# The edge network's first product in float32, from the attributes as they are, with the bias in a row of ones

## The reference

```python
e = jax.nn.relu(ea @ ee_w1 + ee_b1) @ ee_w2 + ee_b2     # ea: 100000 x 64, ee_w1: 64 x 256
msg = x[src] + e
agg = jax.ops.segment_sum(msg, dst, num_segments=n)
```

## Time and profile before

| | value |
|---|---|
| median of three runs | 3226.73 us (3221.56 to 3228.65) |
| profiled execution, and its span | 3227.56 us, 3225.7 us |
| PE busy | 2512.0 us, 78% |
| VectorE (DVE) busy | 2228.2 us, 69% |
| ScalarE (ACT) busy | 1485.7 us, 46% |
| GpSimd (POOL) busy | 2020.3 us, 63% |
| mean granted TensorE clock | 0.903 |
| edge stage, first gather to last | 94.4 to 1098.5 us |

### The profile page before, as it was taken

How to read it: one execution, slowest core, us unless ns; L and a number is a source line. 1 busy time by engine, 2 the same in 40 slices (tenths; PEclk the granted TensorE clock), 3 DMA queues, 4 the chain that set the end, 5 groups by cost and what they waited for, 6 DMA issues and landing times. The chain is left out here.

```text
span 3225.7 us, 81208 instructions
## 1 busy us (share of the span) xinstructions
PE 2512.0 (78%) x25602; PEld 2184.7 (68%) x25603; DVE 2228.2 (69%) x4515; ACT 1485.7 (46%) x3803; POOL 2020.3 (63%) x2143
## 2 busy tenths in 40 slices
PE   0577777777778699999999999965777777777773
PEld 0466666666666589999999999964555555555552
DVE  7687778778777546666666666657666667766666
ACT  5344444444444377888888888841111111111113
POOL 4677777777777534444444444427777777777772
PEclk9998899889888899999999999987998888879886
DMA  6555555555555400000000000006555555655654
GB/s 155 168 159 161 152 160 170 158 158 166 153 160 157 118 7 20 19 19 19 19 19 19 19 19 19 19 23 178 172 171 171 172 172 171 172 171 173 172 171 133
DMA packets 183839, 373.70 MB, mean 116 GB/s; under 512 B 42597, under 2 KB 93687, under 8 KB 183768
## 3 DMA queue, kind: packets, MB, share of 16 engines
q0 software_dynamic: 75552, 209.66, 23.2%
q1 hardware_dynamic: 107392, 162.37, 17.0%
q10 hardware_dynamic: 824, 0.87, 0.1%
HBM read 346.95 MB, written 25.80 MB: 116 GB/s over the span
## 5 line engine op out<-in xcount | busy, mean ns | idle before, releaser
L449 POOL DMA_INDIRECT rows<-tab_scratch,srcs x784 | 766.3, 977 | 238.8 <-issue 231.2
L1438 POOL DMA_INDIRECT a_rows<-tab_scratch,srcs x784 | 751.7, 959 | 252.2 <-issue 235.4
L1504 PE MATMUL sum_ps<-feat,a_hot 128*125 128x264 f32 x1960 | 607.9, 466 | 234.2 <-DVE feat L1596 113.0
L1504 PEld LDWEIGHTS sum_ps<-feat,a_hot 128*125 128x125 f32 x1960 | 421.4, 225 | 341.5 <-issue 131.5
L875 PE MATMUL z_ps<-ah,w 128*128 128x125 f16 x6400 | 554.0, 219 | 0.6 <-PEq L973 0.6
L875 PE MATMUL z_ps<-al,w 128*128 128x125 f16 x3200 | 542.9, 217 | 0.0
L875 PEld LDWEIGHTS z_ps<-ah,w 128*128 128x128 f16 x6400 | 489.9, 97 | 1.0 <-issue 0.9
L1448 ACT ACTIVATE feat<-d 128x32 f32<-128x32 f32 x196 | 44.9, 229 | 827.7 <-DVE d L1592 575.7
L503 PE MATMUL mlp_ps<-ewa,eab 128*128 128x256 f16 x788 | 207.2, 294 | 270.3 <-PEq L499 269.3
L1049 ACT ACTIVATE a<-z,pack 128x125 f32<-128x125 f32 x800 | 321.5, 480 | 145.9 <-ACTq L1045 145.9
L510 PE MATMUL sum_ps<-rows,hot 128*125 128x256 f16 x980 | 295.0, 301 | 66.3 <-DMA rows<-tab_scratch,srcs 34.3
(11 more groups left out here) (206 smaller groups left out, 5609.2 us busy)
## 6 DMA issues: line engine op xcount, KB each, us to landing
ea<-edge_t SPq DMA_DIRECT2D x394, 128.0 KB
dstb<-dst_flat SPq DMA_DIRECT2D x98, 512.0 KB
rows<-tab_scratch,srcs POOLq DMA_INDIRECT x784
a_rows<-tab_scratch,srcs POOLq DMA_INDIRECT x784
tab_scratch<-prow SPq DMA_DIRECT2D x50, 128.9 KB
hx<-x SPq DMA_DIRECT2D x50, 125.0 KB
x_scratch<-x SPq DMA_DIRECT2D x50, 125.0 KB
hs<-tab_scratch SPq DMA_DIRECT2D x50, 125.0 KB
```

The lines of the kernel that those rows point to most:

```text
L449: pool.indirect_dma_start(rows[:, b % DEEP, k, :], None, dram["tab0"], bass.IndirectOffsetOnAxis(ap=srcs[:, c:c + 1], axis=0),).then_inc(r ...
L1438: pool.indirect_dma_start(rows[:, b % DEEP, k, :], None, dram["tab1"], bass.IndirectOffsetOnAxis(ap=srcs[:, c:c + 1], axis=0),).then_inc(r ...
L1504: ins = pe.matmul(out[:], hot[:, h, k, :], feat[:, row, k, :], start=(k == 0), stop=(k == CB - 1))
```

## The change

The attributes are loaded once, in float32, into 64 partitions of `ea`; partition 64 holds ones, written once by DVE. `ewa` is now the float32 weight with the bias as its 65th row, loaded straight to its place. One float32 product for each chunk takes the place of the two float16 products. The split on ACT and DVE, the second load, the buffers and semaphores of the split, the preparation of `ewb`, and POOL's memset of the ones are gone. ACT, and no longer PE, frees `ea`, once the product is done.

```diff
-                for name, shape, dt in [("ewa", [P, D], F16), ("ewb", [ED + 2, D], F16), ("dsts", [P, NCH + CB], F32)]:
+                for name, shape, dt in [("ewa", [ED + 1, D], F32), ("dsts", [P, NCH + CB], F32)]:
...
-            act.dma_start(er[0:ED, :], t["L0_gnn_ee_w1"]).then_inc(ld_small, 16)
-            act.dma_start(er[ED:2 * ED, :], t["L0_gnn_ee_w1"]).then_inc(ld_small, 16)
-            act.dma_start(ebr[0:ED, :], t["L0_gnn_ee_w1"]).then_inc(ld_small, 16)
-            act.dma_start(ebr[ED:ED + 2, :], t["L0_gnn_ee_b1"].partition_broadcast(2)).then_inc(ld_small, 16)
+            act.dma_start(sb["ewa"][0:ED, :], t["L0_gnn_ee_w1"]).then_inc(ld_small, 16)
+            act.dma_start(sb["ewa"][ED:ED + 1, :], t["L0_gnn_ee_b1"].partition_broadcast(1)).then_inc(ld_small, 16)
...
-            act.wait_ge(eb_split, 1)
-            act.sem_inc(eb_split, -1)
-            act.dma_start(sb["ewb"][ED:ED + 1, :], ebh[ED:ED + 1, :]).then_inc(ewb_done, 16)
-            act.wait_ge(ewb_done, 16)
...
-            settled(dve.tensor_copy(sb["ewa"][:], er[:]))
-            settled(dve.tensor_copy(ebh[:], ebr[:]))
-            settled(dve.tensor_tensor(sb["ewb"][:], ebr[:], ebh[:], ALU.subtract))
-            dve.sem_inc(eb_split, 1)
...
-        ea = m.sb("ea", [P, 2, BE], F32)
-        eab = m.sb("eab", [P, 2, BE], F16)
-        eah = m.sb("eah", [ED + 2, 2, BE], F16)
+        ea = m.sb("ea", [ED + 1, 2, BE], F32)
...
                 sp.dma_start(ea[0:ED, s, :], eb).then_inc(ea_ready[s], 16)
-                sp.dma_start(ea[ED:P, s, :], eb).then_inc(ea_ready[s], 16)
...
-            pool.memset(eah[ED:ED + 2, :, :], 1.0).then_inc(ones_ready, 1)
...
-            def high_parts(s):
-                act.wait_ge(ea_ready[s], 32)
-                act.sem_inc(ea_ready[s], -32)
-                act.activation(eab[:, s, :], ea[:, s, :], ACT.Copy).then_inc(ea_high, 1)
-                act.activation(eah[0:ED, s, :], ea[0:ED, s, :], ACT.Copy).then_inc(ea_high, 1)
...
-                    high_parts(1 - s)
                     act.wait_ge(mlp_done, 1)
                     act.sem_inc(mlp_done, -1)
+                    act.sem_inc(ea_free, 1)
...
-                pe.wait_ge(ea_split, 1)
-                pe.sem_inc(ea_split, -1)
-                pe.sem_inc(ea_free, 1)
+                pe.wait_ge(ea_ready[s], 16)
+                pe.sem_inc(ea_ready[s], -16)
                 for k in range(CB):
-                    e = slice(k * P, (k + 1) * P)
-                    pe.matmul(mlp_ps[:, s, k, :], eab[:, s, e], ewa[:], start=True, stop=False)
-                    ins = pe.matmul(mlp_ps[:, s, k, :], eah[:, s, e], ewb[:], start=False, stop=True)
+                    ins = pe.matmul(mlp_ps[:, s, k, :], ea[:, s, k * P:(k + 1) * P], ewa[:], start=True, stop=True)
                 ins.then_inc(mlp_done, 1)
...
-            def low_parts(s):
-                dve.wait_ge(ea_high, 2)
-                dve.sem_inc(ea_high, -2)
-                dve.tensor_tensor(eab[ED:P, s, :], ea[ED:P, s, :], eab[ED:P, s, :], ALU.subtract).then_inc(ea_split, 1)
...
-                    low_parts(1 - s)
                     low_activations(s)
...
+            dve.memset(ea[ED:ED + 1, :, :], 1.0).then_inc(ones_ready, 1)
```

More of the change, by code:

```diff
@@ L128, in prepare @@
         eps1 = m.sb("eps1", [P, 1], F32)
-        er = m.sb("er", [P, D], F32)
-        ebr = m.sb("ebr", [ED + 2, D], F32)
-        ebh = m.sb("ebh", [ED + 2, D], F16)
         stat = m.sb("stat", [TN, NT, 6], F32)
@@ L147, in prepare @@
         consts = m.sem("consts")
-        eb_split, ewb_done = m.sem("eb_split"), m.sem("ewb_done")
         var_ready, sd_ready, coef_ready = m.sem("var_ready"), m.sem("sd_ready"), m.sem("coef_ready")
@@ L195, in _ @@
             pool.memset(acc[:, 0:NT // 2, D:2 * D], 0.0)
-            pool.wait_ge(ld_small, 16 * 6)
+            pool.wait_ge(ld_small, 16 * 4)
             for c in range(CH):
@@ L291, in _ @@
                 settled(dve.tensor_reduce(ext[:, 2 + j:3 + j], drow[:, j, :], AX, ALU.max))
-            dve.wait_ge(ld_small, 16 * 6)
+            dve.wait_ge(ld_small, 16 * 4)
             settled(dve.tensor_scalar(eps1[:], eps1[:], 1.0, None, ALU.add))
-            settled(dve.tensor_copy(sb["ewa"][:], er[:]))
-            settled(dve.tensor_copy(ebh[:], ebr[:]))
-            settled(dve.tensor_tensor(sb["ewb"][:], ebr[:], ebh[:], ALU.subtract))
-            dve.sem_inc(eb_split, 1)
             stats(0)
@@ L349, in edges0 @@
         m = Memory(nc, ctx)
-        acc, iota16, negbase, ewa, ewb = sb["acc"], sb["iota16"], sb["negbase"], sb["ewa"], sb["ewb"]
+        acc, iota16, negbase, ewa = sb["acc"], sb["iota16"], sb["negbase"], sb["ewa"]
         srcs = sb["srcs"]
@@ L379, in edges0 @@
         ones_ready = m.sem("ones_ready")
-        ea_high = m.sem("ea_high")
-        ea_split = m.sem("ea_split")
         mlp_done = m.sem("mlp_done")
@@ L485, in _ @@
             act.sem_inc(w_split, 1)
-            high_parts(0)
             turn()
@@ L538, in body @@
                         sums(sum_ps[:, 2, :], 2, u, s).then_inc(xsum_done, 1)
-                pe.matmul(used_ps[:], ewa[:, 0:1], ewa[:, 0:1], start=True, stop=True).then_inc(r_free, 1)
-                pe.matmul(used_ps[:], ewa[:, 0:1], ewa[:, 0:1], start=True, stop=True).then_inc(rows_free, 1)
+                pe.matmul(used_ps[:], iota16[:, 0:1], iota16[:, 0:1], start=True, stop=True).then_inc(r_free, 1)
+                pe.matmul(used_ps[:], iota16[:, 0:1], iota16[:, 0:1], start=True, stop=True).then_inc(rows_free, 1)
             with pe.Fori(0, FULL) as i:
@@ L616, in _ @@
             dve.sem_inc(chain_sem, -1)
-            low_parts(0)
             def turn(i):
```

## The result

| | kernel before, us | changed kernel, us | ratio, 95% interval |
|---|---|---|---|
| first comparison | 3226.47 (6 runs) | 3240.12 (3224.55 to 3244.69, 6 runs) | 1.0035 [1.0021, 1.0049] |
| second comparison | 3222.14 (14 runs) | 3228.97 (3213.64 to 3233.59, 10 runs) | 1.0009 [0.9992, 1.0026] |

The forecast was 3217, faster. By the first comparison the kernel became 0.35% slower (its interval lies above 1); by the second, 0.1%, no difference can be told.

What follows compares the result with a forecast made beforehand. POOL's row of gathers was taken to set the edge stage's length. Terms -16.5 - 1.1 - 0.5 + 8 = -10.1 from the profiled 3227.6 us gave 3217.5, forecast as 3217, range 3205 to 3240.

Steps and rivals of the forecast that it cites:

- The subtraction goes, and 16.5 us of held gathers with it.: DVE's subtraction in the edge stage holds POOL's gathers; removing it gives -16.5 us, between -21.4 and -11.
- POOL's memset, the opening stage: -1.6.: Before the first gather: -1.1 us for POOL's memset of the ones, -0.5 for the opening stage.
- ACT's conversions and the second load: nothing.: Edge stage: removing ACT's two conversions and the second attribute load gives 0, being in nobody's way.
- The product: +0.92 us at full clock.: PE's float32 product in the edge stage costs +0.92 us a batch at full clock, +1.89 at half, 1.12 mixed.
- A tie at worst, if PE can use its idle time. It can use most: Edge stage: PE would need 5.04 us a batch against POOL's new pace of 5.03, using most of 1.20 idle.
- a lag of 8 us: End of the edge stage: PE finishing later behind POOL costs 8 us, between 0 and 19.
- Where the idle time before line 503 would go: PE before its product: 269.3 of 270.3 us idle were read as the wait for the split, gone after the change.
- The rival "PE becomes the bound": Edge stage: 0.2 us a batch of unusable PE idle time makes the kernel slower, 3244 us; chance 0.22.
- Its signal: For PE as the bound: POOL's idle time before gathers above 240 us, ended by PE's `used_ps`.
- The hold stays: Rival: DVE's next operation holds the gathers instead, so no change, 3228 us; chance 0.12.
- 252 gathers under line 325: Count against the hold staying: 252 gathers passed their early part under line 325, none lasting over 1.02 us.

Runs made afterwards that it cites:

- e2: The kernel before without DVE's subtraction, so the lower half of the attributes is left out: 3206.77 us, ratio 0.9939.
- e1: The changed kernel run once more unchanged, for a second trace (the second comparison): 3228.97 us, ratio 1.0009.
- e9: The changed kernel with one bfloat16 pass in place of the float32 product, precision left out: 3200.05 us, ratio 0.9931.
- e5: The changed kernel without PE's product of the low activations in the edge stage: 3204.17 us, ratio 0.9942.
- e8: The changed kernel with PE's schedule loads once in 12 batches in place of once in 6: 3244.99 us, ratio 1.0070.
- e6: The kernel before with its subtraction on DVE cut in four of 128 columns each: 3216.59 us, ratio 0.9984.

## Why the prediction was wrong, point by point

- *The subtraction goes, and 16.5 us of held gathers with it.* Right in mechanism and size. Held time 23.0 to 5.9 us in the changed kernel, and 15.4 us of the kernel's time in e2 alone.
- *POOL's memset, the opening stage: -1.6.* The first gather starts at 93.6 for 94.4, and at 92.8 in e1: -0.8 of it came in the one trace and -1.6 in the other. What lies between the opening's parts was not tested.
- *ACT's conversions and the second load: nothing.* Not tested by itself on a chip of 3223 us; e9 has both gone, and its last sum ends at 1085.3 beside 1086.2 in e2, which has both: no cost of theirs is seen in the edge stage.
- *The product: +0.92 us at full clock.* Right: 1.97 to 2.00 us for eight records, against 1.06. In busy time it came to less than the 1.12 a batch of the prediction. The product's own went from 232.6 to 416.6 us over the whole stage, +0.93 a batch. PE's total rose less: 896.3 us over (385 + 393) / 4 = 194.5 batches is 4.61 for 3.92, +0.69. The sums became shorter, the mean clock in the stage being 0.92 for 0.895, and records of the product overlap with those beside them.
- *"A tie at worst, if PE can use its idle time. It can use most", and from it a lag of 8 us.* This is the step that failed. PE was busy for less than I gave it, 4.61 us a batch and not 5.04, but 0.51 us a batch of its idle time, which the prediction put at nothing, it could not use: 53.0 us before the product are loads of the schedule, and 45.7 before the sums are waits for DVE, 98.7 / 194.5. Most of it could have been read from the trace of the kernel before: 54.6 us at turn heads right behind the loads, and 27.7 of the 62.5 us before line 510 for the `hot` of a second tile, together 0.42 a batch. Busy and idle make the 5.12 us that a batch took, as it had before, where POOL's own pace would have been 5.03. This sum is the length of the stage over its batches and no measurement of its own; that PE sets the pace is shown by its never waiting for rows, and by e5 and e9. The 0.08 between them are 16 us over 196 batches: POOL waits 16.0 us for the ring in the one trace and 20.5 in the other. The lag came on top: the last sum ends 13.0 and 19.7 us after the last gather, where it was 7.9. From first gather to last sum that makes -0.8 - 17.1 + 16.0 + 5.1 = +3.2, against a measured +2.4 (1106.4 to 1108.8), and +10.8 in the second comparison. The median of the first comparison is 13.7 us over that of the kernel before; none of its slower executions was traced, so how this larger loss is made up stays open.
- *Where the idle time before line 503 would go.* I had read 269.3 us "ended by PEq L499" as the wait for the split, all of it to be had. 101.45 of them lay before PE's first matmul, and of the other 168.9 some 54.6 ended with the sequencer's loads. A wait that is released late hides what would have been late by itself.
- *The rival "PE becomes the bound"* named this: 0.2 us of idle time that cannot be used, "branches, the schedule's loads, waits for `hot` of a second tile", and 3244. It had 0.22. The median was 3240 in the first comparison and 3229 in the second. That the first comes so near its 3244 is in part luck: the idle time that cannot be used was 0.51 and not 0.2, and the busy time 0.43 less than was put beside it. Its signal, POOL's idle time before gathers above 240 us and ended by `used_ps`, is what the trace shows: 263.3, or 254.7 without the 8.6 us before the first gather. e5 and e9 confirm it by giving PE less to do, and e8 by making it pause longer.
- *The hold stays*: refuted by e2 and by the trace after. The count that the prediction set against it, 252 gathers under line 325, comes out at 186 when the instruction running 130 ns after a gather's start is looked up; the longest of them is 1.02 us, so the reading stands.
- The nodes' and second edge stage took 5.3 to 7.7 us less in the traces after than before (from the last sum to the end: 2114.0 and 2111.5 for 2119.3), which is why the profiled span is 2.9 us shorter although the stage ends later. It is no effect of the change that could be told from chance: over the ten traces of this kind of chip this part takes 2107.6 us (e6) to 2120.3 (e2), both of them forms of the kernel before.

## What to carry to other kernels

When work is moved onto an engine that looks idle, its idle time has to be sorted first: what of it ends with the wait that the change removes, and what is the engine's own (register loads at a loop's head, waits for a second engine). Here 1.20 us of idle time a batch looked like room for 1.12, and 0.51 of it was not room at all. Here the two engines came within 2% of one another (5.12 and 5.03 us a batch), and then a gain on one shows only if the other has room: without its subtraction the kernel before gains 15 us, with a float32 product in its place it gains nothing. Values that PE's sequencer loads at run time are better asked for behind queued matmuls than at a loop's head: that takes PE's pauses away (49.3 us to 2.0), though on the chips where it was tried the time fell clearly on one of three.

## What the runs showed of the hardware

- An indirect gather that starts under a VectorE subtraction of two SBUF tensors waits for it to end: all 61 that it held ended 0.82 us after it. Cut into four pieces of 0.24 us the hold halves (23.0 to 11.4 us), and without it it is 7.6.
- A load of values into PE's registers takes 0.30 us for one, 1.47 for six and 2.87 for twelve: 0.23 a value. On VectorE's sequencer six take 0.81 and one 0.31, 0.10 a value. The Trainium skill ("Runtime: NRT & Kernel Launch", Instruction fetch mechanics) gives about 0.2 us a register even in bulk: PE's loads agree, VectorE's are half of it.
- After 1.75 us without work PE came back at 2.4 GHz in the pause shown, and in 37 of the 63 pauses of up to 2.1 us in two traces; after the long pauses of e8 (4.59 us in the one shown) it was at 1.2 GHz in 15 of 17. The eight float32 records take 1.97 us at the one clock and 3.75 at the other.
- The same kernel took 3222 to 3227 us on one kind of chip and 3888 to 3896 on three others, where PE stood idle for 99 to 226 us of the edge stage without a wait that the profile shows, and POOL's idle time over its issue was 239 to 281 us for 0 to 20. The sign of this change is not the same on both.
